# Moving the first tile steps of the last expert stage in between the last operations of the attention before it, and the last softmax denominators to the end

## The reference, cut to what matters

```
x = x + attn_a(layernorm(x))     # one head, rotary positions
x = x + ffn(layernorm(x))        # 8 experts, each token goes to one
x = x + attn_b(layernorm(x))     # 16 heads of 64, causal
x = x + ffn(layernorm(x))        # the same experts again

def ffn(x):
    logits = x @ Wr + br
    idx    = argmax(logits)                  # the expert of each token
    gates  = softmax(logits)[idx]
    for ei in range(8):                      # only tokens with idx == ei count
        h = gelu(x @ W1[ei] + b1[ei]); y = h @ W2[ei] + b2[ei]
        out += y * gates * (idx == ei)
```

## Time and profile before

| | |
|---|---|
| median of 3 runs | 843.16 us (843.04 to 843.72) |
| the profiled execution, its own time | 842.97 us |
| its span, first to last instruction | 841.1 us |
| busy: TensorE, VectorE, ScalarE, GpSimd | 800.6, 620.5, 562.0, 433.6 us |
| mean granted TensorE clock | 0.991 |
| end of call 17's dense part, first routing instruction, last scatter of results | 715.6, 731.43, 827.43 us |

### The profile page before, as it was taken

How to read it: one execution, slowest core, us unless ns; L and a number is a source line. 1 busy time by engine, 2 the same in 40 slices (tenths; PEclk the granted TensorE clock), 3 DMA queues, 4 the chain that set the end, 5 groups by cost and what they waited for, 6 DMA issues and landing times.

```text
span 841.1 us, 22553 instructions
## 1 busy us (share of the span) xinstructions
PE 800.6 (95%) x6857; PEld 692.8 (82%) x6860; DVE 620.5 (74%) x2697; ACT 562.0 (67%) x2028; POOL 433.6 (52%) x755
## 2 busy tenths in 40 slices
PE   8999879999899999999999999999999999899993
PEld 5887749999788888888888888888778888589992
DVE  4889766666667777777877777887767776676765
ACT  2666636666777777777777777777767777356661
POOL 3343737775544544544444444444874544247772
PEclk9999999999999999999999999999999999999997
DMA  9940021431200000000000000000020000003135
GB/s 323 337 132 2 23 89 47 132 96 39 74 2 2 2 2 2 2 2 1 2 2 1 3 2 2 2 2 2 31 95 3 2 2 2 2 23 125 54 102 168
DMA packets 27702, 40.65 MB, mean 48 GB/s; under 512 B 4672, under 2 KB 19904, under 8 KB 26560
## 3 DMA queue, kind: packets, MB, share of 16 engines
q1 hardware_dynamic: 20480, 27.91, 10.3%
q0 software_dynamic: 4992, 10.27, 3.7%
q10 hardware_dynamic: 2112, 1.05, 0.5%
HBM read 20.79 MB, written 18.43 MB: 47 GB/s over the span
## 4 chain that ended last, share of the span: by engine, by line
PE 74%; DVE 10%; POOL 7%; issue 6%; DMA 2%; ACT 1%; DVEq 1%; SPq 0%; POOLq 0%
PE PS L1205 11%; PE PS L1217 10%; PE PS L1196 10%; PE PS L1169 9%; PE PS L1160 9%; PE PS L1248 6%; PE PS L1040 5%; PE PS L1042 5%; PE PS L1041 5%; POOL xs_dram L333 2%; POOL w1b L366 2%; PE PS L1152 1%; POOL pb L392 1%; POOL rstdA L328 1%; POOL pb L390 1%
## 5 line engine op out<-in xcount | busy, mean ns | idle before, releaser
L390 POOL TENSOR_SCALAR pb<-pb,rib 128x128 f32<-128x128 f32 x256 | 95.3, 372 | 251.7 <-DVE rib L920 251.0
L911 DVE CUSTOM_DVE_ANT_0 PS<-PS,CST 128x128 f32<-128x128 f32 (+1 forms) x512 | 169.0, 383 | 60.7 <-PE PS L1217 60.5
L925 DVE COPY pT<-PS 128x384 f32<-128x384 f32 x256 | 140.3, 555 | 37.5 <-PE PS L1196 37.0
L526 ACT ACTIVATE pb<-PS,nbb 128x128 f32<-128x128 f32 x256 | 94.9, 371 | 96.5 <-DVE nbb L911 92.7
L499 ACT ACTIVATE yT<-PS,w1b 128x128 f32<-128x128 f32 x368 | 104.9, 368 | 61.5 <-PE PS L1160 61.5
L392 POOL TENSOR_SCALAR pb<-pb,rib 128x256 f32<-128x256 f32 x256 | 122.3, 478 | 0.0
L1196 PE MATMUL PS<-CST,pb 128*128 128x128 f32 x768 | 117.7, 279 | 4.1 <-POOL pb L392 3.6
L528 ACT ACTIVATE pb<-PS,nbb 128x256 f32<-128x256 f32 x256 | 121.2, 473 | 0.0
L349 POOL DMA_INDIRECT yt_dram<-XY x92 | 92.1, 1001 | 35.9 <-issue 21.9
L1196 PEld LDWEIGHTS PS<-CST,pb 128*128 128x128 f32 x768 | 85.8, 142 | 27.9 <-issue 23.2
L1205 PE MATMUL PS<-pT,vb 128*64 128x256 f32 (+1 forms) x1024 | 103.3, 339 | 2.2 <-DVE pT L925 1.8
(11 more groups left out here) (132 smaller groups left out, 1682.4 us busy)
## 6 DMA issues: line engine op xcount, KB each, us to landing
xs_dram<-XY SPq DMA_DIRECT2D x2, 1483.5 KB, 15.7
XY<-xs_dram SPq DMA_DIRECT2D x2, 1225.5 KB, 6.1
W1S<-in_W SPq DMA_DIRECT2D x1, 2048.0 KB, 20.8
W2S<-in_W SPq DMA_DIRECT2D x4, 512.0 KB, 8.2
xs_dram<-XY SPq DMA_DIRECT2D x1, 1612.5 KB, 10.9
out_dram<-X SPq DMA_DIRECT2D x6, 256.0 KB, 2.4
yt_dram<-XY POOLq DMA_INDIRECT x92, 2.6
xs_dram<-XY SPq DMA_DIRECT2D x1, 1354.5 KB, 11.9
```

Of the source, the lines that this page charges most:

```text
L390: nc.gpsimd.tensor_scalar(pb[:, i, 0:P], pb[:, i, 0:P], rib[:, i, 0:1], 1.0, ALU.mult, ALU.mult)
L911: last = nc.vector.tensor_tensor_reduce(ps, ps, CST[:, m:m + c1 - c0], -SCALE_B, HIGHEST, ALU.add, ALU.min, nbb[:, hh % 4, c0 // P:c0 // P ...
L925: nc.vector.tensor_copy(pT[:, hh % 4, :], PS[:, bank, 0:3 * P]).then_inc(b_pT, 1)
```

## The change

Only the second expert stage is touched. On TensorE and ScalarE the order was: all of attention b, then the routing's part, then steps 0, 1, 2 and so on. It is now: attention b up to call 17, steps 0 to 3, call 18, the further steps; TensorE makes the routing's two products after step 5, and ScalarE takes the routing's exponentials after the last step. VectorE does steps 0 and 1 in the middle of call 17, step 2 behind it, step 3 in the middle of call 18, and weaves the routing into steps 4 to 10, now with 26 instructions: the two of the gates stand behind the last step. GpSimd waits for 26 instead of 28. The three groups of idle products at this place are gone. The pace of the scatters is as it was. In call 18 the router uses another PSUM bank, since the steps have banks 0 to 3 by then. The diff, cut to its core:

```diff
+def once_bank(b):
+    return T_BANK if b == NB - 1 else ONCE_BANK
...
             def before_scatters(k):
-                pool.wait_ge(r_step, STEPS * (k + 1))
+                pool.wait_ge(r_step, STEPS * (k + 1) - (2 if k == 3 else 0))
...  ScalarE, experts
-                route(GROUPS * layer + 1)
-                load_table(ACT.Gelu)
-                expert_steps(step, 0, first_quarter if layer == 0 else None)
+                else:
+                    load_table(ACT.Gelu)
+                    for s in range(4):
+                        step(s, s % RING)
+                    attn_b(NB + 2, 0)
+                    expert_steps(step, 4)
+                    route(3)
...  VectorE
+            def gates(k, done=None):
+                ...
+                dve.wait_ge(r_exp, k + 1)
+                for what in range(2):
+                    if what == 0:
+                        last = nc.vector.reduce_sum(r_den[:, 0:gt], r_ex[:, 0:gt, :], AX.X)
+                    else:
+                        last = nc.vector.reciprocal(GATE[:, t0:t0 + gt], r_den[:, 0:gt])
...  VectorE, route
-                dve.wait_ge(r_exp, k + 1)
-                yield from then(nc.vector.reduce_sum(den, ex, AX.X))
-                yield from then(nc.vector.reciprocal(GATE[:, t0:t0 + gt], den))
+                if k < 3:
+                    yield from gates(k, done)
...  VectorE, experts
+                    routing, parts = parts, iter(())
+                    step(0, 0)
+                    step(1, 1)
+                    attn_b(NB + 1, 1, 2, QUADS)
+                    step(2, 2)
+                    attn_b(NB + 2, 0, 0, 2)
+                    step(3, 3)
+                    attn_b(NB + 2, 0, 2, QUADS)
+                    parts = routing
+                    first, woven = 4, 4 + -((2 - STEPS) // 4)
...
+                if layer == 1:
+                    for _ in gates(3):
+                        pass
...
-            peeled(attn_b, ROUTE2_AT + 3, 19)
+            peeled(attn_b, ROUTE2_AT + 3, NB + 1)
+            attn_b(NB + 1, 1, 0, 2)
             experts(1)
...  TensorE, experts
-                keep_clock((20, 0)[layer], 4)
-                step(0, 0)
-                step(1, 1)
-                step(2, 2)
-                keep_clock((6, 10)[layer], 4)
+                else:
+                    for s in range(4):
+                        step(s, s % RING)
+                    attn_b(NB + 2, 0)
+                    step(4, 0)
+                    step(5, 1)
+                    route(3)
+                    expert_steps(step, 6)
...  TensorE, attn_b
-                        router(gb + NB, v, ONCE_BANK)
-                        if fixed(s) and s >= NB + 1:
-                            keep_clock((11, 10)[s - (NB + 1)], T_BANK)
+                        router(gb + NB, v, once_bank(gb))
...
-AHEAD = (18, 0)
+AHEAD = 18
```

More of the change, by code:

```diff
@@ L501, in step @@
                         last.then_inc(f_gelu, 1)
-                route(GROUPS * layer + 1)
-                load_table(ACT.Gelu)
-                expert_steps(step, 0, first_quarter if layer == 0 else None)
+                if layer == 0:
+                    route(1)
+                    load_table(ACT.Gelu)
+                    expert_steps(step, 0, first_quarter)
+                else:
+                    load_table(ACT.Gelu)
+                    for s in range(4):
[3 more added lines that the diff above has]
+                    route(3)
             def first_quarter(i):
@@ L555, in attn_b @@
                     if q == 1 and has(gb):
-                        router_copy(gb + NB, v, ONCE_BANK)
+                        router_copy(gb + NB, v, once_bank(gb))
                     if q == 3 and has(s):
@@ L584, in _ @@
             attn_b(ROUTE2_AT, ROUTE2_AT % 2, 1, QUADS)
-            peeled(attn_b, ROUTE2_AT + 1, 19)
+            peeled(attn_b, ROUTE2_AT + 1, NB + 2)
             experts(1)
@@ L737, in attn_a @@
                 part()
+            def gates(k, done=None):
+                t0, gt = GT0[k], GTS[k]
+                done = done or [STEPS * (k + 1) - 2]
+                dve.wait_ge(r_exp, k + 1)
[4 more added lines that the diff above has]
+                        last = nc.vector.reciprocal(GATE[:, t0:t0 + gt], r_den[:, 0:gt])
+                    done[0] += 1
+                    last.then_inc(r_step, 1)
+                    yield
+                    dve.wait_ge(r_step, done[0])
             def route(k):
@@ L773, in route @@
                                              ALU.is_equal))
-                dve.wait_ge(r_exp, k + 1)
-                yield from then(nc.vector.reduce_sum(den, ex, AX.X))
-                yield from then(nc.vector.reciprocal(GATE[:, t0:t0 + gt], den))
+                if k < 3:
+                    yield from gates(k, done)
                 dve.wait_ge(r_pre_ps, k + 1)
                 yield from then(nc.vector.tensor_copy(ps, PS[:, ROUTE_PLACES[k][0], ROUTE_PLACES[k][1]:ROUTE_PLACES[k][1] + 2 * E * gt]))
-                assert done[0] == STEPS * k + READ_STEP
+                assert done[0] == STEPS * k + READ_STEP - (2 if k == 3 else 0)
                 pre = e_t(r_ps[:, 0:E * gt])
@@ L813, in route @@
                 yield from then(nc.vector.tensor_scalar(TE[:, NJ0[k]:NJ0[k] + nj], te, float(E - 1), None, ALU.min))
-                assert done[0] == STEPS * (k + 1), done[0]
+                assert done[0] == STEPS * (k + 1) - (2 if k == 3 else 0), done[0]
             def experts(layer):
@@ L863, in step @@
                         nc.vector.tensor_copy(xs1[:, w, :], XY[:, ds(j), 0:D]).then_inc(f_in, 1)
[L866 to L869, removed]
+                if layer == 0:
+                    for _ in range(AHEAD):
+                        next(parts)
+                    first, woven = 0, -((AHEAD - STEPS) // 4)
+                else:
[9 more added lines that the diff above has]
+                    first, woven = 4, 4 + -((2 - STEPS) // 4)
+                for s in range(first, woven):
                     step(s, s % RING)
@@ L977, in attn_b @@
                     if q == 2 and has(gb):
-                        logits(gb + NB, TPB * gb, ONCE_BANK)
+                        logits(gb + NB, TPB * gb, once_bank(gb))
                     if q == 3 and has(s):
@@ L1171, in step @@
                         last.then_inc(f_y_ps, 1)
-                route(GROUPS * layer + 1)
-                keep_clock((20, 0)[layer], 4)
-                step(0, 0)
-                step(1, 1)
-                step(2, 2)
-                keep_clock((6, 10)[layer], 4)
-                expert_steps(step, 3, first_quarter if layer == 0 else None)
+                if layer == 0:
+                    route(1)
+                    keep_clock(20, 4)
+                    step(0, 0)
+                    step(1, 1)
+                    step(2, 2)
+                    keep_clock(6, 4)
+                    expert_steps(step, 3, first_quarter)
+                else:
+                    for s in range(4):
[5 more added lines that the diff above has]
+                    expert_steps(step, 6)
             def first_quarter(i):
@@ L1273, in attn_b @@
                         wait(pe, r_lg, gb + NB)
[L1274 removed]
+                        router_T(gb + NB, once_bank(gb))
                     if q == 2 and has(gb):
[L1276 to L1278 removed]
+                        router(gb + NB, v, once_bank(gb))
                     if q == 3 and has(s):
```

## The result

The kernel after takes 848.13 us (847.51 to 848.75, 4 runs) against 843.12 us: ratio 1.0054, 95% interval 1.0041 to 1.0067. It is slower by 5.0 us, on the side that had 0.62, but twice as much as the 2.5 us of the forecast. It lies inside the range that was given (842.5 to 848.5) by 0.4 us only, and outside the forecast's own (844.9 to 847.0).

A forecast was written before the change was run, and what follows sets the result against it. Group 3's scatters and gather, started by the routing's end, were taken to bound the gain. 842.97 + 1.0 (tile 23 late) + 1.5 (clock) = 845.5 us profiled, 845.7 median; forecast's own range 844.9 to 847.0, given range 842.5 to 848.5.

The forecast's parts named there:

- the side that had 0.62: The predicted outcome that the kernel after is slower by over 0.2%, given a chance of 0.62.
- What bounds the stage: Second expert stage: four steps, 7.6 us, gained only as far as group 3's scatters and gather come forward; GpSimd's queue next.
- Steps 0 to 2, normalisation: VectorE around call 17: steps 0 and 1 cost nothing, step 2 moves the normalisation from 728.95 to 729.5.
- Tile 0 ahead of call 18: TensorE and ScalarE do tile 0's products and Gelu before the router: logits 1.8 us late, routing starts at 733.2.
- The routing in full steps: Routing woven into steps 4 to 10, with a wait at step 5: lasts 15.4 us, ends at 748.6.
- The wait for tile 23: VectorE waits 4 us for group 3's gather and copies tile 23 at 778.2, 1.0 us late.
- The clock behind tile 23: TensorE's clock falls to half in or just behind the wait at tile 23, costing 1.5 us, bounds 0 and 3.
- Idle products gone: Hand-over: the removed idle products lay in waits and cost no time; a clock fall could delay routing about 1 us.
- rival 2: The clock falls in the hand-over too, since idle products are gone: about 1.3 us more, 847.0; chance 0.15.
- Exponentials and gates at the end: Moved behind the last step, they fit in VectorE's 5.31 us wait for the first results gather: nothing, otherwise 2.2 us.

The follow-up runs named there:

- e4: The kernel after, but VectorE waits at tile 23 only for group 3's small transfer and at tile 27 for the large one; 845.48 us, ratio 1.0019.
- e10: The kernel after with idle products back in the hand-over and group 3 waited for by its two transfers; 842.39 us, ratio 0.9992 to the kernel before.
- e12: The kernel after with tile 0's work earlier, hand-over idle products, group 3 waited for by two transfers, four routing instructions per step; 840.10 us, ratio 0.9965.
- e1: The kernel after with idle products put back on TensorE in the hand-over (11 after step 2, 4 in call 18); 846.12 us, ratio 1.0035.
- e9: The kernel after with idle products in the hand-over and at tile 23, and tile 0's work done before call 18's router; 842.19 us, ratio 0.9993.
- e2: The kernel after with 16 idle products on TensorE ahead of its wait for input tile 23; 846.95 us, ratio 1.0043.
- e3: The kernel after with idle products both in the hand-over and ahead of the wait for tile 23; 844.77 us, ratio 1.0018.

## Why the prediction was right in kind and short in size

**What bounds the stage.** Right that group 3 bounds it, and GpSimd's queue behind that: e4, e10 and e12 show the second bound. The wait at tile 23, 3.7 us for a predicted 4, agrees by chance in the kernel after. Predicted was VectorE at 774.1 with a lead of 3 us over the kernel before, and the copy at 778.2; measured were 777.1, no lead at all, and 780.86. Both ends are about 3 us late, and so are the routing's end (751.8 for 748.6) and the last result tile (832.35 for 829 to 830). In e1 the mechanism is as predicted: tile 22 is copied 3.4 us ahead of the kernel before from the logits, and the wait of 4.7 us gives it back.

**Steps 0 to 2, normalisation.** Right: the normalisation starts at 729.53 (predicted 729.5), steps 0 and 1 cost nothing. From the logits it is 0.7 us late, for the 0.55 of the prediction.

**Tile 0 ahead of call 18.** Right where the clock is up: the chain is 2.0 us longer in e1 (6.6 against 4.6), 1.8 were predicted. e9, which takes exactly these operations out of the chain, has 4.6 again. The mechanism is shown for these operations together.

**The routing in full steps.** 15.3 us in e1, from 732.92 to 748.19, for a predicted 15.4; the wait for TensorE's products behind step 5 is 0.68 us there for 0.6. Its first scatter at 748.47 stands against the predicted 748.9.

**GpSimd.** It starts 0.3 us after the routing, as taken from the first stage. Its 16 scatters took 20.7 us, I had taken 21.3. The large transfer, taken as 6.3 us, landed after 6.6 in the kernel after and 7.5 in e1; e2 to e4 and e9 to e12 have 6.1 to 7.6.

**The wait for tile 23.** From the first scatter to the copy 28.8 us in the kernel after and 29.7 in e1, predicted 29.3.

**The clock behind tile 23.** 1.3 us in the profile and 1.35 between the medians of e1 and e3, predicted 1.5. The page of the Trainium skill, "TensorE: Matmul & The Clock Gate", section "HAM oscillation — how this bites in real kernels", said that a dense stream which waits in between starts again at the low clock. The trace agrees, with 1.00 in the windows of the wait and 0.52 and 0.50 in those from 781 us, where the products start again; e2 and e3, which fill the wait, keep 1.00.

**The step that failed** is "Idle products gone", which stood in the sum at nothing and was left to rival 2 with 0.15 and 1.3 us. The clock fell in the hand-over in the kernel after, in e2 and in e4, every profile without the idle products there, and in none with them. The low stretch was 10.2, 6.8 and 6.8 us long. The earlier trace rows have 3.4, where the prediction reads 3.2: the 0.60 of the window from 106 us puts the fall at 106.2 and not 106.4. Rival 2 had the mechanism but was mis-sized, because I counted only tile 0's products at half speed. In e4 these weren't even slow (1.06 us). The stretch went on over the router product and step 4's two groups into step 5's, and so over the wait of the routing there. Its cost was 3.3 us of first scatter in the kernel after and 1.7 in e2 and e4, and 2.0 to 2.2 us of median (the kernel after against e1, e2 against e3). With that in place of nothing the sum of 845.7 would be 847.7 to 847.9; the median was 848.13. What makes the stretch 6.8 us long in one execution and 10.2 in another, no run shows.

**Exponentials and gates at the end.** Right: they end at 833.6, and the first results of the last transfer are used at 838.51. They cost nothing here. What moving them gained was not tested by itself.

## What to carry to other kernels

Work that is moved into the idle time of a chain is free only if no engine of the chain must finish it first: look at what then stands ahead of the chain's next operation in each in-order queue. Before filling TensorE's idle time with real work in place of idle products, look whether the granted clock stays up in the stretch, since what it loses there comes back where another engine waits for TensorE. And when a stage is started earlier, find the transfers and the slower queue that feed or drain it; here waiting per transfer, with the lead of the early steps kept and the routing hardly later than before (e12), gave 3 us, while the early steps as first written cost 5, and their lead was gone before it could be used.

## What the runs showed that I had not expected

The low clock of the hand-over lasted 6.8 to 10.2 us although TensorE worked through most of it (busy 1.00 in most windows from 730 to 740 us in the kernel after), while behind tile 23 it was over after 3.4 us. And one session ran the same kernel before at 894 us. The profiles of its four other kernels show three engines stopping together; nothing in their rows names the cause.
